# Graph attention in fp32 on one core: softmax blocks cut by key modulo four, and values used without a re-ordered copy

## The reference

```python
q, k, v = (proj(Wq, bq), proj(Wk, bk), proj(Wv, bv))      # (b, 8 heads, 256, 32)
scores = jnp.einsum('bhqd,bhkd->bhqk', q, k) * SCALE      # SCALE = 32 ** -0.5
mask = (adj_matrix + bond_matrix)[:, None, :, :]          # both are adj
attn = jax.nn.softmax(scores * mask, axis=-1)
ctx = jnp.einsum('bhqk,bhkd->bhqd', attn, v)
y = jnp.einsum('bse,fe->bsf', ctx, Wo) + bo
out = layernorm(x + y)
```

## Time and profile before

| | |
|---|---|
| median of 3 runs | 414.3 us (414.0 to 415.63) |
| profiled execution, its own time | 411.37 us |
| span of the profiled execution | 409.4 us |
| busy: TensorE, VectorE, ScalarE, GpSimd | 93%, 90%, 88%, 67% |
| mean busy share of the 16 DMA engines | eight to nine tenths in nearly every slice |
| mean granted TensorE clock | 0.979 of full speed |

### The profile page before, as it was taken

How to read it: one execution, slowest core, us unless ns; L and a number is a source line. 1 busy time by engine, 2 the same in 40 slices (tenths; PEclk the granted TensorE clock), 3 DMA queues, 4 the chain that set the end, 5 groups by cost and what they waited for, 6 DMA issues and landing times.

```text
span 409.4 us, 12272 instructions
## 1 busy us (share of the span) xinstructions
PE 382.1 (93%) x3628; PEld 294.2 (72%) x3628; DVE 370.4 (90%) x1335; ACT 359.0 (88%) x1224; POOL 273.0 (67%) x507
## 2 busy tenths in 40 slices
PE   8997999999899979999999989799999999988692
PEld 7764777777678857778777767677777778866471
DVE  3997799999989969999999998969999999999765
ACT  4699899999899959999999979959999999999750
POOL 3252557786777756787777866747677877556665
PEclk9998999999999989999999999989999999999988
DMA  8478877988988888999888889889998988887803
GB/s 268 136 199 236 218 217 200 257 210 255 257 231 241 223 212 264 272 259 251 242 215 239 254 244 254 217 230 239 263 246 259 233 219 232 236 216 215 229 27 103
DMA packets 65428, 92.30 MB, mean 225 GB/s; under 512 B 8529, under 2 KB 48722, under 8 KB 65362
## 3 DMA queue, kind: packets, MB, share of 16 engines
q1 hardware_dynamic: 47426, 66.35, 63.4%
q10 hardware_dynamic: 17936, 25.17, 18.3%
HBM read 26.22 MB, written 8.39 MB: 85 GB/s over the span
## 4 chain that ended last, share of the span: by engine, by line
PE 62%; SPq 12%; ACT 8%; DVE 7%; DMA 5%; issue 4%; POOL 2%; DVEq 0%; ACTq 0%; POOLq 0%
PE proj_bank L334 16%; PE row_bank L265 11%; PE ctx_bank L405 11%; SPq L209 7%; PE out_bank L422 7%; PE out_bank L352 7%; ACT probs L729 6%; PE turn_bank L282 5%; DMA carried<-boxes 4%; SPq L218 3%; DVE boxes L538 3%; PE turn_bank L367 2%; DVE probs L525 2%; PE turn_bank L454 1%; DVE context L553 1%
## 5 line engine op out<-in xcount | busy, mean ns | idle before, releaser
L729 ACT ACTIVATE probs<-probs,low_top 128x256 f32<-128x256 f32 x512 | 254.8, 509 | 4.4 <-POOL low_top L937 4.4
L525 DVE CUSTOM_DVE_ANT_0 probs<-row_bank,adj_rows 128x256 f32<-128x256 f32 x512 | 181.5, 420 | 13.5 <-PE row_bank L265 10.7
L538 DVE STREAM_TRANSPOSE boxes<-probs 128x1536 f32<-128x1536 f32 x62 | 109.6, 1767 | 0.0
L729 ACT ACTIVATION_READ_ACCUMULATOR probs<-probs,low_top 128x1 f32 x512 | 102.6, 200 | 0.0
L334 PE MATMUL proj_bank<-xt_parts,w_parts 128*128 128x512 f32 x360 | 99.9, 413 | 0.0
L334 PEld LDWEIGHTS proj_bank<-xt_parts,w_parts 128*128 128x128 f32 x360 | 63.2, 189 | 33.7 <-issue 22.5
L937 POOL TENSOR_SCALAR low_top<-top 128x4 f32<-128x4 f32 x128 | 25.5, 199 | 88.7 <-issue 51.4
L265 PE MATMUL row_bank<-kq 32*128 32x256 f32 x1024 | 73.8, 402 | 0.2 <-DVE top L525 0.2
L405 PE MATMUL ctx_bank<-carried,v_boxed 128*32 128x256 f32 x744 | 63.5, 402 | 8.1 <-DMA carried<-boxes 7.9
L405 PEld LDWEIGHTS ctx_bank<-carried,v_boxed 128*32 128x32 f32 x744 | 29.8, 113 | 35.7 <-issue 21.7
L265 PEld LDWEIGHTS row_bank<-kq 32*128 32x128 f32 x1024 | 46.5, 184 | 12.5 <-issue 6.2
(11 more groups left out here) (86 smaller groups left out, 448.0 us busy)
## 6 DMA issues: line engine op xcount, KB each, us to landing
carried<-boxes SPq DMA_DIRECT2D x248, 192.0 KB, 4.3
xt<-in_x_t SPq DMA_DIRECT2D x32, 256.0 KB, 4.5
adj_rows<-in_adj ACTq DMA_DIRECT2D x32, 256.0 KB, 4.9
xr<-in_x ACTq DMA_DIRECT2D x32, 256.0 KB, 4.2
v_boxed<-v SPq DMA_DIRECT2D x124, 64.0 KB, 3.1
out<-result ACTq DMA_DIRECT2D x31, 256.0 KB, 5.1
w_whole<-in_wk ACTq DMA_DIRECT2D x2, 128.0 KB, 3.6
w_whole<-in_wq SPq DMA_DIRECT2D x1, 256.0 KB, 4.3
```

The source lines that it names most:

```text
L525: last = nc.vector.tensor_tensor_reduce(probs[:, h % RING, t * S:(t + 1) * S], row_bank[j][:, t * S:(t + 1) * S], adj_rows[:, (g // 2) % 2 ...
L538: nc.vector.transpose(boxes[:, n % BOXES].rearrange("p a h (f q) -> p (h f) a q", q=D), probs[:, first:first + BOXED, :].rearrange("p h (f ...
L729: last = nc.scalar.activation(tile, tile, ACT.Exp, bias=low_top[:, g % 2, J * c + j, t:t + 1], accum_out=sums[:, g % 2, t, j * T + c:j * T ...
```

## The change

The reading pattern of the block transpose is changed. A block now holds every fourth key of a tile (keys a, 4 + a, 8 + a, ...) instead of 32 neighbours. The result still goes to the same places in `boxes` and `carried`, so partition 4k + a of `carried` now holds key 4k + a of the tile, as in `v`. All heads are multiplied with `v`. `v_boxed`, `carry_v`, its semaphores `v_in` and TensorE's wait on them are removed. In `probs`, the innermost 32 elements that the transpose reads were 4 bytes apart and are now 16 bytes apart; it reads the same 1536 elements of each partition and writes them in the same order as before.

```diff
-        v_boxed = sb("v_boxed", [P, 2, 2, T, E])
...
-            def carry_v(n):
-
-                sp.wait_ge(v_ready, n + 1)
-                wait(sp, ctx_made, n - 3)
-                for j in range(J):
-                    sp.dma_start(v_boxed[j::J, (n // 2) % 2, n % 2].rearrange("p t e -> p (t e)"),
-                                 v[D * j:D * (j + 1), (n // 2) % 2, n % 2].rearrange("p t e -> p (t e)")
-                                 ).then_inc(v_in[n % 4], 16)
...
-            carry_v(0)
...
-                if 0 <= g + 1 < LAST:
-                    carry_v(g + 1)
...
             def weigh_v(g):
                 pe.wait_ge(v_ready, g + 1)
-                if g < LAST:
-                    pe.wait_ge(v_in[g % 4], 64 * (g // 4 + 1))
...
-                                                    values[:, (g // 2) % 2, g % 2, t, o * D:(o + 1) * D], tile, start=(t == 0),
+                                                    v[:, (g // 2) % 2, g % 2, t, o * D:(o + 1) * D], tile, start=(t == 0),
...
                 nc.vector.transpose(boxes[:, n % BOXES].rearrange("p a h (f q) -> p (h f) a q", q=D),
-                                    probs[:, first:first + BOXED, :].rearrange("p h (f a k) -> p (h f) a k", a=J, k=D)
+                                    probs[:, first:first + BOXED, :].rearrange("p h (f k a) -> p (h f) a k", a=J, k=D)
                                     ).then_inc(boxed, 1)
```

More of the change, by code:

```diff
@@ L103, in build @@
         stored = [sem(f"stored{n}") for n in range(2)]
-        x_in, adj_in, v_in, carried_in = (
-            [sem(f"{name}{n}") for n in range(4)] for name in ("x_in", "adj_in", "v_in", "carried_in"))
+        x_in, adj_in, carried_in = (
+            [sem(f"{name}{n}") for n in range(4)] for name in ("x_in", "adj_in", "carried_in"))
         xt_in = [[sem(f"xt_in{n}_{t}") for t in range(T)] for n in range(2)]
@@ L394, in weigh_v @@
                             if g == LAST:
-                                values = v
                                 tile = last_tile(c, j)[:, t * S:(t + 1) * S].rearrange("p (u i q) -> p u i q", u=T, i=J)
                             elif j < BOXED:
-                                values = v_boxed
                                 tile = carried[:, g % 2, c, :, j, :].rearrange("p i (u t q) -> p t u i q", u=T, t=T)[:, t]
                             else:
-                                values = v
                                 tile = turned_probs[:, (2 * g + c) % 4, t * S:(t + 1) * S]
```

## The result

The changed kernel takes 466.19 us (median of 4 runs, 465.4 to 466.64) against 414.15 us for the kernel before beside it. The ratio is 1.125, with a 95% interval of 1.121 to 1.130. I had forecast 402 us and put 0.45 on slower. The range of 399 to 504 holds the time; the direction was wrong. Over all its runs, here and beside the experiments, the kernel before took 411.2 to 426.9 us, the longer ones mostly at a lower granted clock, and the ratios are of its undisturbed runs alone.

What follows compares the result with a forecast made beforehand. TensorE was taken to bound the kernel at 11.41 us a graph, VectorE close behind. Products 0, transpose 0 and stalls -11.6 us took own time from 411.4 to 399.8; with run surplus, 402 us, range 399 to 504.

Steps and rivals of the forecast that it cites:

- Who paces, and the stalls: TensorE sets the 11.41 us period; removing the values' transfers from SP's full queue ends stalls worth 11.6 us.
- the 2.9 us that I carried over: Median of the runs shown above the profiled execution, added to the forecast's own time of 399.8 us, giving 402.7.
- `v` for `v_boxed` and the wait removed: TensorE's products with `v` and its dropped wait on `v_in`: zero, as products take the same 379 ns.
- I take zero as the value, narrowly: VectorE's transpose reading 16 bytes apart, two a graph: stays at 1767 ns, no added time.
- my bounds of 0 and 2.1: Added time of each transpose: at least nothing, at most 2.1 us, from GpSimd's subtraction at 2.50 ns an element.
- VectorE's room: VectorE's slack under TensorE's period, taken as 0.16 us a graph.
- The slower rival with a doubled element time: Each VectorE transpose grows by 1.57 us, VectorE sets the period, runs 495 to 503 us; chance 0.33.
- the half price: Rival: half an element's time, 0.8 us a transpose on VectorE, period 12.85 us, runs 448 us; chance 0.09.
- a part of the price: Rival case: VectorE's transpose read pays part of a doubled element time, runs 415 to 487 us; chance 0.09.
- the break-even: Growth of each VectorE transpose that would cancel the whole gain: 0.27 us (1767 ns to 2040).
- The queue: SP's issuing queue: removal frees about 3 to 4 us a graph, worth only the stalls, nothing in good periods.

Runs made afterwards that it cites:

- e2: Changed kernel with the contiguous transpose read of before, still without the values' copy and transfers: 399.01 us, ratio 0.960 to the kernel before.
- f2: Kernel before with the values' copy sent once for two graphs, same bytes in about half as many transfers: 398.49 us, ratio 0.961.
- f4: Changed kernel with the stride of four split into two 8-byte steps, in mask-and-maximum and transpose: 398.10 us, ratio 0.962 to the kernel before.
- e1: Kernel before with only the strided transpose read put in, values' copy and transfers kept: 465.32 us, ratio 1.120 to the kernel before.
- The quiet row: Kernel before with single instructions of different strides run alone behind its last store: the transpose read at 16 bytes costs 1.11 us more.
- e4: Changed kernel with the transpose reading every third instead of every fourth element, 12 bytes apart: 424.45 us.
- f3: Changed kernel with the stride moved from the transpose's read to the mask-and-maximum's write, for three heads: 433.15 us.

## Why the prediction was wrong

- **Who paces, and the stalls: right.** TensorE's 11.4 us a graph is the floor of e2, f2 and f4 alike. The 11.6 us of long periods came from the queue (f2), and their removal took the span to 397.2 us (forecast 397.8). The median fell further, to 399.0: the 2.9 us that I carried over from before had no place in e2, whose runs lie between 398.9 and 400.2. That the surplus of before was more stalls is likely by this, and not shown, as no trace of a longer run of before was kept.
- **`v` for `v_boxed` and the wait removed: right,** nothing to see in e2.
- **The step that failed: "I take zero as the value, narrowly"**, for the transpose's read. It measured 1.28 us (1767 to 3048 ns), inside my bounds of 0 and 2.1 but far from the end I chose. The reason given was that the transpose of before "shows an engine bound by its element rate and not by the layout". That row could not show it: its reads lie side by side and its writes run over 32 neighbours before they jump, so the row says nothing of a jump at every element. What the runs showed in place of the zero is a price of 0.83 ns an element in the kernel, 0.72 when quiet, from 16 bytes of distance on; 2 x 1.28 us is far more than VectorE's room, so VectorE took over the period, and e1 shows that this is the whole slowdown. The right reading was that no row priced it.
- **The page that spoke against the change.** The Trainium skill's "SBUF — State Buffer", Specifications, states lines of 16 bytes, of which two accesses each are needed for full bandwidth. The quiet row agrees at each distance: 8 bytes free (1779 ns), 12 in part (2219), 16 and more alike (2747 to 2921). The Trainium skill's "VectorE: DVE Perf Modes", Mode 1× (REGULAR), which I set against it, says that fp32 and "weird strides" work in that mode; it names no time, and 2885 ns against 1778 shows that working is not the same as being free.
- **The rivals' sums.** The slower rival with a doubled element time gave 495 to 503 and the half price 448; the measured 466.2 lies between, as 1.28 does between 1.57 and 0.8. The case that came true, a part of the price with 415 to 487 us, had a chance of only 0.09. The arithmetic was off in one more term: I took VectorE's room as 0.16 us a graph from its busy time, and e4 shows 0.3. Why the busy time overstates VectorE's work by 0.15 us a graph no run shows. So the break-even was about 0.41 us a transpose and not 0.27.
- **The queue.** That its relief is worth nothing once VectorE is the bound was in the rival (VectorE sets the period, and TensorE's stalls are hidden), and e1 shows it.

## What to carry to other kernels

Look at the bytes between neighbouring elements of each access pattern on VectorE and ScalarE in SBUF. In fp32, VectorE's reads 8 bytes apart were free here. Reads 16 bytes apart cost 0.7 to 0.9 ns an element on VectorE and ScalarE, and on VectorE 24, 32 and 64 bytes cost no more. Writes paid too: 0.7 ns at 16 bytes, 0.5 at the 256 bytes of f3. A stride of four can be made of two strides of two in instructions that run anyway (f4). An issuing queue is a resource with a period of its own: add up its issues per round before trusting slack elsewhere, and merge small transfers (f2) before redesigning data. And where a row of the profile has no instance of an access, it must not be read as evidence that the access is free.

## What was not expected of the hardware

- A transpose that reads 16 bytes apart takes longer beside TensorE (3.06 us from start to start, 18.38 / 6) and ScalarE (2.97) than alone (2.91), and not beside transfers (2.91).
- A price below one more element time: 16 bytes apart makes a transposed element 1.75 ns when quiet, (2885 - 200) / 1536, instead of 1.02, and not 2.04.
- ScalarE read PSUM 16 bytes apart in 586 ns for 512 elements, the same as side by side, while from SBUF it took 1088 instead of 617.
